# Attention with weight and decay taken from one PSUM bank, and a GpSimd tile write ahead of each gather

## What is computed

```python
f_src, f_dst, f_v = feat @ W_src.T + b_src, feat @ W_dst.T + b_dst, feat @ W_v.T + b_v
a = f_src[src] + f_dst[dst]
e = where(a >= 0, a, 0.2 * a)
ex = exp(e - segment_max(e, dst)[dst])
rst = segment_sum(f_v[src] * ex / segment_sum(ex, dst)[dst], dst)
```

## Time and profile before

| | us |
|---|---|
| median of the three runs | 4121.9 |
| the profiled execution's own time | 4101.72 |
| its span (first to last instruction) | 4099.9 |
| first gather of a chunk's rows starts at | 2467.09 |
| first gather of the result rows starts at | 3787.86 |

### The profile page before, as it was taken

The page is one execution under the profiler, slowest core; times in us unless marked ns, Lnnn a source line. Parts: engine busy times, 40 slices in busy tenths (PEclk is TensorE's granted clock), DMA queues, the critical chain, the costliest instruction groups (busy, mean ns, idle before and its releaser), DMA issues.

```text
span 4099.9 us, 37229 instructions
## 1 busy us (share of the span) xinstructions
PE 2542.5 (62%) x10401; PEld 1326.1 (32%) x10549; DVE 1919.4 (47%) x4040; ACT 1070.9 (26%) x2573; POOL 1597.2 (39%) x1664
## 2 busy tenths in 40 slices
PE   0211211111114668789577557999999999998198
PEld 0000100000001123344222214666666666665044
DVE  3545654444442223311310305777777777776510
ACT  0533233333331000100100002444444444444100
POOL 0566266666664000110000026555555556554100
PEclk6555655555556998899899758999999999999597
DMA  9950391000006992033299316787788778876142
GB/s 385 377 202 2 129 370 35 2 2 2 2 2 224 408 403 108 0 118 107 98 326 326 132 59 194 234 242 236 238 242 243 238 238 246 241 236 193 49 150 70
DMA packets 466664, 728.61 MB, mean 178 GB/s; under 512 B 70249, under 2 KB 340628, under 8 KB 466560
## 3 DMA queue, kind: packets, MB, share of 16 engines
q1 hardware_dynamic: 389396, 611.92, 43.1%
q0 software_dynamic: 65680, 109.05, 10.1%
q10 hardware_dynamic: 11484, 6.49, 0.5%
HBM read 444.96 MB, written 282.31 MB: 177 GB/s over the span
## 4 chain that ended last, share of the span: by engine, by line
PE 45%; DVE 20%; issue 15%; DMA 12%; another core or an unknown queue 4%; ACT 2%; POOL 1%; ACTq 1%; SPq 0%; DVEq 0%; POOLq 0%
DMA G<-adj_d 11%; DVE G L1250 8%; PE PS L576 7%; DVE G L1251 6%; PE PS L746 5%; PE PS L770 4%; PE PS L775 4%; PE PS L802 4%; PE PS L804 4%; PE PS L803 4%; PE PS L769 2%; PE PS L754 2%; PE PS L837 1%; PE PS L719 1%
## 5 line engine op out<-in xcount | busy, mean ns | idle before, releaser
L510 POOL DMA_INDIRECT adj_d<-D,place x782 | 751.1, 961 | 540.3 <-issue 216.7
L504 POOL DMA_INDIRECT G<-tab_sv,src_e x784 | 753.9, 962 | 532.7 <-issue 282.5
L1250 DVE SCALAR_TENSOR_TENSOR G<-PS,G 128x256 bf16<-128x256 f32 x782 | 355.4, 480 | 309.1 <-issue 144.4
L619 PE MATMUL PS<-OSF,onesb 3*128 3x512 bf16 x200 | 101.2, 611 | 550.1 <-DVE G L1251 352.8
L1447 DVE TENSOR_TENSOR_SCAN RB<-mring,RB,PS 128x512 f32<-128x512 bf16 x196 | 251.2, 1282 | 156.0 <-PE PS L775 80.1
L1035 ACT ACTIVATE G<-PS 128x512 f32<-128x512 f32 x196 | 117.1, 597 | 673.5 <-DVE G L1251 539.3
L545 POOL DMA_INDIRECT run_d<-V,head_i x25 | 24.0, 961 | 666.5 <-ACT V L1124 659.2
L770 PE MATMUL PS<-VT 128*128 128x128 f32 x1568 | 274.4, 277 | 0.0
L976 ACT ACTIVATE OSF<-PS 128x512 f32<-128x512 f32 x392 | 212.9, 596 | 219.6 <-PE PS L576 216.7
L769 PE MATMUL PS<-ident,G 128*128 128x128 f32 x784 | 216.1, 276 | 65.2 <-issue 56.7
L1427 DVE TENSOR_TENSOR_SCAN HTx<-PS,HTx,D 128x512 f32<-128x512 f32 x196 | 250.3, 1277 | 4.4 <-PE PS L576 3.6
(11 more groups left out here) (322 smaller groups left out, 4391.6 us busy)
## 6 DMA issues: line engine op xcount, KB each, us to landing
G<-adj_d SPq DMA_DIRECT2D x350, 512.0 KB
frac_d<-OSF SPq DMA_DIRECT2D x196, 512.0 KB
adj_d<-RB SPq DMA_DIRECT2D x7, 12800.0 KB, 59.3
run_d<-RB SPq DMA_DIRECT2D x4, 12992.0 KB
VT<-run_d SPq DMA_DIRECT2D x196, 256.0 KB
mring<-cut_d SPq DMA_DIRECT2D x196, 128.0 KB
HTx<-seg_d SPq DMA_DIRECT2D x196, 128.0 KB
OSF<-cnt_d SPq DMA_DIRECT2D x42, 512.0 KB
```

The costliest lines, as they stand in the source:

```text
L504: pool.indirect_dma_start(dest, None, table, bass.IndirectOffsetOnAxis(ap=idx, axis=0)).then_inc(done, 16)
L510: pool.indirect_dma_start(adj_d, bass.IndirectOffsetOnAxis(ap=place[:, 2 * w + k:2 * w + k + 1], axis=0), pay[:, w, k, :], None).then_inc( ...
L1250: v.scalar_tensor_tensor(junk[:, w % 2, k, :], PS[:, bank, c], off_f[:, 2 * w + k:2 * w + k + 1], wrow[:, s, c], ALU.is_equal, ALU.mult, a ...
```

## The change

The running maximum itself is computed as before. With u = e - (m_prev + cut), built in bank q, the weight is exp(-relu(-u)) and the decay exp(-relu(u)). So TensorE adds only -RB (shifted by one: m_prev) and -cut to bank q, ScalarE makes both relu from that bank, and then both exponentials. ScalarE waits for its own two relu (`gx`) ahead of the exponentials; `weighted` on VectorE waits for a new semaphore `gp`, raised by the second exponential. The write of bank 4 + q moves from TensorE to ScalarE, and with it goes TensorE's wait for `gback` of chunk c - 2. On GpSimd each gather of the pass has a memset of a 128 x 128 f32 tile `beat_t` ahead of it, which nobody reads; each memset waits for the one before (`beaten`). The chunk's waits for `ga` and `gv` stand ahead of its first memset.

```diff
-        identb = sb("identb", [P, P], bf16)
+        nidentb = sb("nidentb", [P, P], bf16)
...
+        beat_t = sb("beat_t", [P, P])
...
+            def beat():
+
+                if beats["n"]:
+                    pool.wait_ge(beaten, beats["n"])
+                pool.memset(beat_t[:, :], 0.0).then_inc(beaten, 1)
+                beats["n"] += 1
...
                     for k in range(CT):
                         t = c * CT + k
+                        beat()
                         rows_of(G[:, h, k, :], tab_sv, src_n[:, t:t + 1], ggath[h])
...
-                        if not (first and h < 2):
-                            pe.wait_ge(gback, GB * (c - 2) + GB)
-                        nc.tensor.matmul(PS[:, 4 + q, :], ident[:, :], RB[:, q * CE:(q + 1) * CE], start=True, stop=False)
-                        nc.tensor.matmul(PS[:, 4 + q, :], nident[:, :], RB[:, q * CE + 1:(q + 1) * CE + 1], start=False, stop=False)
-                        nc.tensor.matmul(PS[:, q, :], nident[:, :], RB[:, q * CE + 1:(q + 1) * CE + 1], start=False, stop=True, skip_group_check=True)
-                        nc.tensor.matmul(PS[:, 4 + q, :], identb[:, :], mring[:, h, :], start=False, stop=True).then_inc(dif, 1)
+                        nc.tensor.matmul(PS[:, q, :], nident[:, :], RB[:, q * CE:(q + 1) * CE], start=False, stop=False, skip_group_check=True)
+                        nc.tensor.matmul(PS[:, q, :], nidentb[:, :], mring[:, h, :], start=False, stop=True, skip_group_check=True).then_inc(dif, 1)
...
                         act.wait_ge(dif, c + 1)
-                        nc.scalar.activation(PS[:, 4 + q, :], PS[:, 4 + q, :], ACT.Exp)
                         if not (first and h < 2):
                             act.wait_ge(gback, GB * (c - 2) + GB)
-                        nc.scalar.activation(D01[:, q, CE:2 * CE], PS[:, q, :], ACT.Exp).then_inc(gx, 1)
+                        nc.scalar.activation(D01[:, q, CE:2 * CE], PS[:, q, :], ACT.Relu, scale=-1.0)
+                        nc.scalar.activation(PS[:, 4 + q, :], PS[:, q, :], ACT.Relu).then_inc(gx, 1)
+                        act.wait_ge(gx, c + 1)
+                        nc.scalar.activation(D01[:, q, CE:2 * CE], D01[:, q, CE:2 * CE], ACT.Exp, scale=-1.0)
+                        nc.scalar.activation(PS[:, 4 + q, :], PS[:, 4 + q, :], ACT.Exp, scale=-1.0).then_inc(gp, 1)
...
-            step(v.tensor_copy(identb[:, :], ident[:, :]))
+            step(v.tensor_copy(nidentb[:, :], nident[:, :]))
...
                     q = h % 2
-                    dve.wait_ge(gx, c + 1)
+                    dve.wait_ge(gp, c + 1)
                     dve.wait_ge(gv, c + 1)
```

More of the change, by code:

```diff
@@ L230, in build @@
         opened = sem("opened")
+        beaten = sem("beaten")
         sgr = [[sem(f"sgr{h}{k}") for k in range(2)] for h in range(2)]
@@ L291, in build @@
         gx = sem("gx")
+        gp = sem("gp")
         gfront = sem("gfront")
@@ L504, in rows_of @@
                 pool.indirect_dma_start(dest, None, table, bass.IndirectOffsetOnAxis(ap=idx, axis=0)).then_inc(done, 16)
+            beats = {"n": 0}
+            def beat():
[3 more added lines that the diff above has]
+                beats["n"] += 1
             def scatter():
```

## The result

The changed kernel takes 4241.97 us (median of four runs, 4195.47 to 4264.8) against 4127.22 for the kernel before beside it (4109.05 to 4136.43). The forecast was 3967 us and faster: wrong in size and in sign. Later the same kernel gave 1.032 on a second chip (h3) and 0.957 on a third (f1).

The account below looks back on a forecast made before the run. PE bounds the kernel at 6.30 us per chunk; then GpSimd would: 784 x 1.46 = 1144.6 us plus about 21 ends the pass 155 us earlier. 4101.7 - 155 = 3947, with the median 20 above: 3967 us; range 3860 to 4160.

Parts of the forecast that it names:

- POOL becomes the bound, and its stretch is counted by gathers: GpSimd in the attention pass: 784 gathers at 1.46 us, 1144.6 us from 2467.09, the last issued at 3611.7.
- occasional late chunks: Kernel before, attention pass: explains the 0.26 us between PE's 6.30 us per chunk and the mean of 6.56.
- PE's floor: TensorE: two f32 matmuls fewer save 1.72 us per chunk, so its floor falls from 6.30 to 4.58 us.
- ScalarE: Two relu and two exponentials replace two exponentials: 1.18 us more, 3.94 us per chunk, lying beside other work.
- VectorE's wait for the exponentials: `weighted` waiting for the later decay and weight: costed at nothing, at most 98 us if the cover fails.
- The memset: GpSimd, ahead of each gather: 0.20 us paid in full, pitch 1.46 us; by start spacing the pitch would be 1.40.
- The break of overlap: Rival on GpSimd: each memset makes gather preparation start anew, pitch 1.91 us, 4319 us; chance 0.18.
- The clock: PE's granted clock in the pass: stays near 2.4 GHz with PE busy 78%; over 0.95 expected.
- The end of the pass: From the last gather to the result gathers: about 21 us instead of 35.4, with only one chunk behind.
- The memset hides: Rival on GpSimd: memsets vanish in the 0.30 us pause between gathers; put at 3880 us; chance 0.14.
- The ring of DVE and ACT: Rival: `weighted` waits for later exponentials and loads come late, 0.35 us lost per chunk, 4037 us; chance 0.10.
- the two signs that would have made the whole wrong: In the pass: a granted clock near 0.5, or PE still at 95%.

Follow-up runs that it names:

- h3: The changed kernel unaltered, run again on a chip of the first kind against the kernel before: 4196.98 us, ratio 1.0321.
- f1: The changed kernel unaltered, run again on a chip of the second kind against the kernel before (3695.78 us): 3534.32 us, ratio 0.9572.
- g1: The kernel before, unaltered, run for its trace on a chip of the first kind: 4067.95 us, ratio 0.9991.
- f3: The changed kernel without the memset ahead of each gather, on a chip of the second kind: 3462.70 us, ratio 0.9360 to the kernel before.
- h2: The changed kernel without mask and segment-mark loads after the first four chunks, on a chip of the first kind: 4197.08 us, ratio 1.0287 to the kernel before.

## Why the prediction was wrong

**The step that failed** is the one behind "POOL becomes the bound, and its stretch is counted by gathers": that a signal of PE arrives when its matmul ends, however densely GpSimd gathers. On the chips of the first kind it doesn't. The evidence was in the earlier trace rows, but not in all of what I read there. Of the 128.0 us of "remote" ahead of L969, 61.8 are the first chunk's wait. The 158.1 ahead of L985 are 80 waits of at most 3.0 us, and they are ordinary waits for PE: that trace has a record of the matmul L805, for which ScalarE waits there, in only 98 of the 196 chunks (all 196 weight loads are there), and without the record the profile cannot name PE. The trace of g1, the same kernel with all 196 records, shows it (engine line waited for: us in total, times, longest us):

```profile
ACT PS L985 <- PE PS L805: 396.0, 181, 2.2
...
ACT M L969 <- remote: 36.1, 9, 5.3
...
ACT PS L985 <- remote: 4.7, 7, 0.9
```

What is left are 66 us in 19 waits ahead of L969. I took them for "occasional late chunks" and carried nothing of them into the sum. They belong to the same holds, 30 in the pass and 56 us late in all, about the 196 x 0.26 = 51 us that PE's work left unexplained. They were kept few and short (8 over 3 us) by the microsecond in which GpSimd stood still for PE. The change removed that microsecond. What GpSimd's wait was worth never got a term.

**PE's floor**, 4.58 us: right. In the three traces of the change (after, h3, f1) the fastest tenth of the chunks takes at most 4.57 to 4.64 us, counted from one relu (L978) to the next.

**ScalarE**, 3.94 us per chunk: 575.62 / 150.6 = 3.82. The wait for its own `gx`, taken at 0.24, costs 6.2 us in 196 chunks ahead of L999, so nothing. No table load was added to the one before.

**VectorE's wait for the exponentials**, costed at nothing: 8.9 us in the pass ahead of L1431, and 7.9 in f1. Right.

**The memset**: not 0.20 but 0.08 us. From one memset to the next are 3003.66 - 3002.33 = 1.33 us, against 1.25 from gather to gather: the memset of 0.22 starts as the gather ends, and the pause to the next gather shrinks from 0.30 to 0.16. f3 against f1 gives 0.091. The 1.40 worked out from the spacing of the memsets was nearer than my 1.46; by this case's rows the rule of the Trainium skill (Perfetto Trace Analysis, GPSIMD Engine Instruction), to time GpSimd by starts, is the better one, and still high. The break of overlap, the slower rival with its pitch of 1.91, did not happen: the result was slower for another reason, and the 4319 us that it gave stand near the 4242 only by chance.

**The clock**, kept at 0.95 or more: right on the second kind (0.97) and wrong on the first, where PE stands idle for 4 to 5 us at a time (0.85 in the change, 0.87 in h3).

**The end of the pass**, 21 us from the last gather to the AH gathers: 24.0 in f1 (3186.7 to 3210.71). In the profiled execution of the change it was 35.4 (3909.3 to 3944.68), as before.

**The sum on a chip of the second kind**: the forecast was a ratio of 3967 / 4121.9 = 0.962, measured 0.957. That is partly two misses that cancel. The gathers' pitch there is (3186.7 - 2112.8) / 783 = 1.37 us instead of 1.46; and since no trace shows the kernel before on such a chip, its pass there is only an estimate: 3695.78, less the 2145 us at which the pass begins in the eight traces there (first relu at 2127 to 2160, the mean is 2145) and the 329 after the last relu in f1, leaves about 1222 us, so 6.23 us per chunk, near PE's floor of 6.30 without a hold. Against that the saving was bound to be smaller than against the 1282 us that the pass takes from first to last relu in the trace of before.

**The rivals.** "The memset hides" came nearest in mechanism (pitch 1.33, DMA share 0.93 in f1). The ring of DVE and ACT did not appear. None of the rivals was a signal that comes late, and the range of 3860 to 4160 excluded what happened. Of the two signs that would have made the whole wrong, neither was there: PE was at 74% and not at 95, and the granted clock was 0.85 over the pass, with 0.50 in a short stretch like the one behind the hold shown above.

## What to carry to other kernels

Idle time released by "remote" while GpSimd issues indirect DMAs can be a signal that was held. First see whether the instruction waited for has its records in the trace (here half of one group's were missing, and 158 us of ordinary waits stood under "remote"); price what is left, and ask what keeps it small. Where an engine is relieved that others were stopped by, the stop may have been worth something; here a microsecond of standing still per chunk was worth more than 1.72 us of PE. If gathers become the pace, a pause of about a microsecond after each four of them can be worth its time, and has to be timed on more than one chip: three memsets ahead of a chunk were a little faster than the kernel before on both kinds (0.977 and 0.986, both intervals below 1), while the change as it was made gives 1.02 to 1.03 on one and 0.957 on the other, and the fastest version on one kind (0.936, no memsets) is the slowest on the other (1.039).

## What was not expected of the hardware

Two kinds of chips. On three sets, and in the first comparison, the kernel before has medians of 4070 to 4127 us; on two sets 3696 and 3705, with identical code. On the second kind hardly a signal was late (0 or 1 holds in 192 chunks in each of the eight traces). The attention pass starts there at about 2140 us instead of 2480, so most of the 370 us between the kinds lie ahead of the pass, where GpSimd scatters 782 times; whether these are holds too wasn't tried. The second kind isn't faster in everything: the stores that zero adj_d take 74 us to land there and 59 on the first.

Held signals come free some 3 us after GpSimd's last gather ends in the wlast stage (0.8 us in h2), and in the pass of the change 2.2 us after the start of the last one (the median over the holds of more than 3 us; 2.7 in e1), several at a time. What holds them, why it takes more than a few gathers in a row to begin, and which property of a chip decides it, stays open. So does whether a gather with fewer rows would hold less; it wasn't tried.
